# Layer 0 attention: softmax denominators of two key blocks in one four-band product, added and spread once per group of heads

## What is computed

```python
q = layer_norm(x) @ Wq                 # 16 heads of 64, 512 queries, 2 batches
k, v = split(layer_norm(ctx) @ Wkv)    # 1024 keys
k = apply_rope(k, cos, sin)
attn = softmax(q @ k.T * 64 ** -0.5)   # exp(scores) / sum over the 1024 keys
x = x + (attn @ v) @ Wo + bo
```

## Time and profile before

| | |
|---|---|
| runs | 3860.3, 3867.1, 3866.78 us; median 3866.78 us |
| the profiled execution | 3865.0 us, of which the span of the trace is 3863.3 us |
| TensorE (PE) busy | 2639.0 us, 68% of the span |
| VectorE busy | 2407.8 us, 62% |
| ScalarE busy | 1475.5 us, 38% |
| mean granted TensorE clock | 0.83 |
| TensorE in layer 0's attention, 91.1 to 610.9 us | 517.17 us busy of 519.80, clock 1.00 |

### The profile page before, as it was taken

One profiled execution on the slowest core, in us unless ns is written; L12 is line 12 of the kernel. 1 busy time (PEld: TensorE's weight loads), 2 busy tenths in 40 slices (PEclk: granted clock), 3 DMA queues, 4 the chain that ended last, 5 costly groups with the idle time before them and its releaser, 6 DMA issues. The chain is left out here.

```text
span 3863.3 us, 39157 instructions
## 1 busy us (share of the span) xinstructions
PE 2639.0 (68%) x11814; PEld 1688.4 (44%) x11814; DVE 2407.8 (62%) x4807; ACT 1475.5 (38%) x2242; POOL 320.4 (8%) x143
## 2 busy tenths in 40 slices
PE   2999996352433322234899995878768598499678
PEld 2444443230111111113788883545433587245367
DVE  4677663848777778873555453665555455587277
ACT  2444441116666766763222212222125122156221
POOL 0000000010000000000222210111110011200021
PEclk8999998575666656666999997889879798789789
DMA  1000000050000000000111101000041110522011
GB/s 56 13 12 13 11 6 35 0 178 6 22 23 23 1 23 22 22 1 32 49 49 49 41 14 41 1 0 0 10 134 42 37 43 17 183 48 67 19 37 35
DMA packets 46338, 136.44 MB, mean 35 GB/s; under 512 B 8568, under 2 KB 18816, under 8 KB 41600
## 3 DMA queue, kind: packets, MB, share of 16 engines
q1 hardware_dynamic: 46208, 135.01, 11.7%
HBM read 106.28 MB, written 28.31 MB: 35 GB/s over the span
## 5 line engine op out<-in xcount | busy, mean ns | idle before, releaser
L1403 ACT ACTIVATE l1a_over_s<-l1a_sc_s,l1a_ntau_s 128x1024 bf16<-128x1024 f32 x272 | 312.2, 1148 | 149.4 <-DVEq L1431 141.4
L1229 PE MATMUL ps<-ident,l1a_worst_s 128*1 128x128 f32 x8 | 3.0, 372 | 484.8 <-DVEq L1490 484.8
L1722 PE MATMUL ps<-m1e_x_part_s,m1e_up_part_s 128*128 128x512 f32 x1296 | 299.1, 392 | 22.0 <-POOL m1e_up_part_s L1818 15.9
L1284 DVE MAX8 l1a_cand_s<-ps 128x8 f32<-128x128 f32 x1024 | 218.4, 284 | 133.2 <-PE ps L1189 127.2
L1722 PEld LDWEIGHTS ps<-m1e_x_part_s,m1e_up_part_s 128*128 128x128 f32 x1296 | 244.5, 189 | 74.5 <-issue 23.7
L1189 PE MATMUL ps<-l1a_ka_s,l1a_qa_s 128*128 128x512 f32 x256 | 146.0, 590 | 110.9 <-ACT l1a_sc_s L1355 90.1
L1355 ACT ACTIVATE l1a_sc_s<-ps 128x512 f32<-128x512 f32 x256 | 153.0, 598 | 168.4 <-DVE l1a_cand_s L1284 168.4
L1229 PEld LDWEIGHTS ps<-ident,l1a_worst_s 128*1 128x1 f32 x8 | 0.6, 79 | 491.6 <-issue 428.7
L1765 ACT ACTIVATE m1e_act_out_s<-ps 128x512 f32<-128x512 f32 x108 | 64.6, 598 | 348.0 <-PE ps L1722 348.0
L973 DVE TENSOR_REDUCE l3a_shift_s<-ps 128x1 f32<-128x1024 f32 x128 | 150.1, 1219 | 65.5 <-PE ps L890 65.5
L543 DVE TENSOR_SCALAR l0a_probs_s<-l0a_probs_s 128x1024 f32<-128x1024 f32 x128 | 88.5, 691 | 150.3 <-ACT l0a_probs_s L610 149.9
(11 more groups left out here) (515 smaller groups left out, 5854.7 us busy)
## 6 DMA issues: line engine op xcount, KB each, us to landing
m1ew_up_s<-m_up SPq DMA_DIRECT2D x9, 1536.0 KB, 6.5
l1a_ka_s<-l_k_parts SPq DMA_DIRECT2D x16, 512.0 KB, 7.8
l3h_ka_s<-l_k_parts SPq DMA_DIRECT2D x16, 512.0 KB, 8.1
m1ew_down_s<-m_down SPq DMA_DIRECT2D x9, 768.0 KB, 4.3
l0a_w_s<-l_w SPq DMA_DIRECT2D x16, 384.0 KB, 3.0
m3ew_up_s<-m_up SPq DMA_DIRECT2D x6, 768.0 KB, 4.2
l_v_groups<-l1p_v_all_s SPq DMA_DIRECT2D x2, 2048.0 KB, 6.6
l1a_qa_s<-l_q_parts SPq DMA_DIRECT2D x16, 256.0 KB, 5.9
```

What stands on the lines that cost most here:

```text
L1284: ins = nc.vector.max(T["cand"][:, r, 8 * (c + j * 4):8 * (c + j * 4) + 8], ps[:, f % 2, c * P:(c + 1) * P])
L1403: nc.scalar.activation(T["over"][:, :], T["sc"][:, r, :], ACT.Relu, bias=T["ntau"][:, r:r + 1], accum_out=T["total"][:, r:r + 1]).then_inc ...
L1722: ins = nc.tensor.matmul(ps[:, 2 * (u % 2) + way, :], up_parts[a][:, k, way, c, :], x_parts[b][:, k, half * BANK:(half + 1) * BANK], start ...
```

## The change

A product with ones as weights is no longer made for each block, but for each second one. After the value product of an odd block t, four products with 32 columns each (L483 after) write four bands of 32 partitions of bank 7: block t-1 of head 0, block t-1 of head 1, block t of head 0, block t of head 1. At the group's end bank 7 holds for each head two partial sums, each 32 times. ScalarE copies it to `den` as before. Then a new product (`denominators`, L490 after) with the constant table `pair_sum` adds the two bands of a head and spreads the sum over the head's 64 partitions, into bank 7 again. It stands in step 2 of the next group, behind the value product of block 0 and ahead of the scores of block 3. The reciprocal reads bank 7 in place of `den`. Its step is FINISH_AT = 3 instead of 6. The value product of block 1, also in step 3, waits for this reciprocal (`rden_ready`), since the bank is written again behind it. The ring of `probs` has 8 places instead of 4, and `pv_done` is raised by two for each second block. `constants` makes `pair_sum` with one memset and two selects on GpSimd.

```diff
+            pool.memset(pair_sum[:, :], 0.0).then_inc(filled, 1)
...
+            both = pair_sum[:, :].rearrange("p (h c) -> p h c", h=2)
+            for part in range(2):
+                pool.wait_ge(made, 5 + part)
+                pool.affine_select(out=both, in_=both, compare_op=ALU.not_equal, fill=1.0, base=-64 * part,
+                                   pattern=[[-32, 2], [0, 64]], channel_multiplier=1).then_inc(made, 1)
...
-            dve.wait_ge(made, 5)
+            dve.wait_ge(made, 7)
...
-    SLOTS = 4
+    SLOTS = 8
...
-    LOW_QUERIES_AT, ROTATE_AT, LOW_KEYS_AT, FINISH_AT = 1, (2, 4), (5, 6), 6
+    LOW_QUERIES_AT, ROTATE_AT, LOW_KEYS_AT, FINISH_AT = 1, (2, 4), (5, 6), 3
...
                 if t == 0:
                     pe.wait_ge(v_ready, 2 * n + 4)
                     pe.wait_ge(o_copied, n + 1)
-                    pe.wait_ge(den_copied, n + 1)
+                if t == 1:
+                    pe.wait_ge(rden_ready, n + 1)
                 pe.wait_ge(clip_done, NC_ * n + t + 1 + SLOTS)
                 for h in range(2):
-                    nc.tensor.matmul(ps[64 * h:64 * h + 64, 6, :], v[:, p, t, 64 * h:64 * h + 64],
+                    ins = nc.tensor.matmul(ps[64 * h:64 * h + 64, 6, :], v[:, p, t, 64 * h:64 * h + 64],
                                      probs[:, t % SLOTS, h * NQ:(h + 1) * NQ], start=(t == 0), stop=(t == NC_ - 1))
-                for h in range(2):
-                    ins = nc.tensor.matmul(ps[64 * h:64 * h + 64, 7, :], ones[:, 0:64],
-                                           probs[:, t % SLOTS, h * NQ:(h + 1) * NQ], start=(t == 0), stop=(t == NC_ - 1))
-                ins.then_inc(pv_done, 1)
+                if t % 2 == 1:
+                    for i in range(4):
+                        ins = nc.tensor.matmul(ps[32 * i:32 * i + 32, 7, :], ones[:, 0:32],
+                                               probs[:, (t - 1 + i // 2) % SLOTS, i % 2 * NQ:(i % 2 + 1) * NQ],
+                                               start=(t == 1), stop=(t == NC_ - 1))
+                    ins.then_inc(pv_done, 2)
+
+            def denominators(n):
+                pe.wait_ge(den_copied, n + 2)
+                nc.tensor.matmul(ps[:, 7, :], pair_sum[:, :], den[:, :], start=True, stop=True).then_inc(den_made, 1)
...
+                    if last is not None and t == 2:
+                        denominators(n - 1)
                 if after is None:
                     value_product(n, p, NC_ - 2)
                     value_product(n, p, NC_ - 1)
+                    denominators(n)
...
                 dve.wait_ge(o_done, n + 1)
-                dve.wait_ge(den_copied, n + 2)
-                nc.vector.reciprocal(rden[:, :], den[:, :]).then_inc(rden_ready, 1)
-                dve.wait_ge(rden_ready, n + 1)
+                dve.wait_ge(den_made, n + 1)
+                nc.vector.reciprocal(rden[:, :], ps[:, 7, :]).then_inc(rden_ready, 1)
+                dve.wait_ge(rden_ready, n + 2)
```

More of the change, by code:

```diff
@@ L94, in link, with constants @@
         self.wait()
-def constants(nc, ident, ones, slot_sum, slot_pick, spread):
+def constants(nc, ident, ones, slot_sum, slot_pick, spread, pair_sum):
     with Stage(nc, "const") as s:
@@ L111, in _ @@
             pool.memset(spread_f32[:, :], 0.0).then_inc(filled, 1)
-            pool.wait_ge(filled, 5)
+            pool.memset(pair_sum[:, :], 0.0).then_inc(filled, 1)
+            pool.wait_ge(filled, 6)
             pool.affine_select(out=ident[:, :], in_=ident[:, :], compare_op=ALU.not_equal, fill=1.0, base=0,
@@ L343, in _, with rope_attention @@
             dve.wait_ge(added, TQ)
-def rope_attention(nc, name, ps, ones, q_t, ctx_t, w_dram, cos_dram, sin_dram, o_all):
+def rope_attention(nc, name, ps, ones, pair_sum, q_t, ctx_t, w_dram, cos_dram, sin_dram, o_all):
     DH = 64
@@ L390, in rope_attention @@
         pv_done = s.sem("pv_done")
-        o_copied, den_copied = s.sem("o_copied"), s.sem("den_copied")
+        o_copied, den_copied, den_made = s.sem("o_copied"), s.sem("den_copied"), s.sem("den_made")
         rden_ready, o_done = s.sem("rden_ready"), s.sem("o_done")
@@ L467, in value_product @@
                     pe.wait_ge(o_copied, n + 1)
-                    pe.wait_ge(den_copied, n + 1)
+                if t == 1:
+                    pe.wait_ge(rden_ready, n + 1)
                 pe.wait_ge(clip_done, NC_ * n + t + 1 + SLOTS)
                 for h in range(2):
-                    nc.tensor.matmul(ps[64 * h:64 * h + 64, 6, :], v[:, p, t, 64 * h:64 * h + 64],
+                    ins = nc.tensor.matmul(ps[64 * h:64 * h + 64, 6, :], v[:, p, t, 64 * h:64 * h + 64],
                                      probs[:, t % SLOTS, h * NQ:(h + 1) * NQ], start=(t == 0), stop=(t == NC_ - 1))
-                for h in range(2):
-                    ins = nc.tensor.matmul(ps[64 * h:64 * h + 64, 7, :], ones[:, 0:64],
-                                           probs[:, t % SLOTS, h * NQ:(h + 1) * NQ], start=(t == 0), stop=(t == NC_ - 1))
-                ins.then_inc(pv_done, 1)
+                if t % 2 == 1:
[7 more added lines that the diff above has]
+                nc.tensor.matmul(ps[:, 7, :], pair_sum[:, :], den[:, :], start=True, stop=True).then_inc(den_made, 1)
             def first():
                 for sem, free in ((w_free, 2), (v_ready, 2), (exp_done, 2), (clip_done, SLOTS), (pv_done, SLOTS),
-                                  (o_copied, 1), (den_copied, 1), (o_done, 1)):
+                                  (o_copied, 1), (den_copied, 1), (o_done, 1), (rden_ready, 1)):
                     nc.tensor.sem_inc(sem, free)
@@ L2510, in build @@
         slot_pick, spread = sb("slot_pick", [P, 60]), sb("spread", [P, 6, P], F32R)
+        pair_sum = sb("pair_sum", [P, P])
         x = sb("x_rows", [P, TQ, D])
@@ L2515, in by_feature @@
             return A[name + "_f"]
-        constants(nc, ident, ones, slot_sum, slot_pick, spread)
+        constants(nc, ident, ones, slot_sum, slot_pick, spread, pair_sum)
         load_x(nc, A["x"], x)
@@ L2555, in build @@
                 o_all = sb("l0_o_all", [P, 8, NT], stack=l0)
-                rope_attention(nc, "l0a", ps, ones, q_t, c_t, A["l0_w"], A["l0_cos"], A["l0_sin"], o_all)
+                rope_attention(nc, "l0a", ps, ones, pair_sum, q_t, c_t, A["l0_w"], A["l0_cos"], A["l0_sin"], o_all)
                 project_out(nc, "l0o", ps, o_all, 8, A["l0_wo"], A["L0_xattn_bo"], x)
```

## The result

The changed kernel takes 3973.96 us (median; 3971.59 to 3977.46), the kernel before, on the same chip, 3865.1 us: a ratio of 1.0284 with a 95% interval of 1.0266 to 1.0302. The forecast was 3980 us.

A forecast was written before the change was run, and what follows sets the result against it. TensorE was taken to bound layer 0's attention. TensorE savings -39.6, new wait +113, slow clock +38 and the rest +1.7 sum to +113 us: 3980 us, 2.9% more, range 3940 to 4000.

The forecast's parts named there:

- the bands: TensorE's denominator products, layer 0 attention: 64 dropped in even blocks save 58.2 us, 64 four-band ones in odd blocks lose 5.8.
- the slow clock: TensorE behind each stop: mean 5.1 us at half pace, 2.6 us lost per gap, +38 us in all.
- spread product, 15 in the stage: TensorE's product adding the bands and spreading the sum: 0.85 us each, 15 inside the stage, +12.8 us.
- TensorE's stop: Value product of block 1 waits for VectorE's reciprocal: 7.7 us in groups 1 to 14, 5.2 in group 15, +113 us.
- constants and the last spread: GpSimd's memset and two selects, 0.7 us, and the last group's bare spread product, 1.0 us: together +1.7 us.
- nothing else is late: The second rotation's result is ready before TensorE asks in step 6, 10.1 against 12.4 us after restart: no second wait.
- Rival (a): After TensorE's stall the clock stays at 2.4 GHz, so the wait costs less: 3942 us; chance 0.10.
- price of a change of band width: On TensorE, 0.05 us more where one product's band width differs from the next one's.
- estimate of 1.08 us for four bands: A four-band product's time from the notes' 2.38 times for three bands; sum 6 us higher; forecast used the trace's 0.99.
- Rival (b): TensorE never feels the wait because the reciprocal is done by 233: faster, 3829 us; chance 0.05.
- turning point: The stall at which faster turns to slower: 2.4 us a group, clock included.
- Rival (c): The four bands don't run together, each pair taking its own 0.91 us: +58 us, 4038 us; chance 0.03.

The follow-up runs named there:

- bands alone: The changed kernel without spread product and new wait, bands copied and reciprocal in step 6, a head's two partial sums not added: 3825.58 us, 0.9892 of before.
- stop filled: The changed kernel with eight extra unneeded 128x512 products in TensorE's wait, groups 1 to 15: 3952.16 us, 1.0225 of before.
- earlier reciprocal: The changed kernel with reciprocal and its multiplication behind the clip of block 2, ahead of the first rotation on VectorE: 3883.48 us, 1.0046 of before.
- later wait: The changed kernel with the wait for the reciprocal moved from the value product of block 1 to the denominator product behind it: 3965.04 us, 1.0255 of before.
- bunched version: The changed kernel with denominator products of four blocks together behind blocks 3 and 7, the wait there, reciprocal in step 3: 3829.85 us, 0.9917 of before.
- narrow product alone: The kernel before with each denominator product of two 64-column bands written as four of 32, nothing merged: 3885.0 us, 1.0047 of before.
- copying versions: The changed kernel with ScalarE copying bank 7 out, the wait on that copy, reciprocal in step 6: 3834.4 us; also with four blocks' denominators together: 3833.15 us.
- half of the stop filled: The changed kernel with four extra unneeded products in TensorE's wait, 4.2 us of idle time left: 3977.97 us, 1.0287 of before.

## Why the prediction was right

The direction, the place, the mechanism and the size came out. Two terms were off, the bands by 10 us and the slow clock by 8.5, in opposite senses: that the total came within 6 us of the median is in part luck, though either error alone would have left it inside the range.

| term | forecast | measured |
|---|---|---|
| bands (even blocks less, odd blocks more) | -52.4 | -42.4 (bands alone, stage end) |
| spread product, 15 in the stage | +12.8 | +12.9 (0.86 each) |
| TensorE's stop | +113 | +111.4 |
| slow clock behind it | +38 | +29.5 (stop filled) |
| constants and the last spread | +1.7 | +2.2 (1.0 and 1.23) |
| the stage | +113 | +113.6 from the parts, +114.9 in the trace |

- **The stop** was the main step, and it held in each piece: 7.60 us for 7.7 in the groups of the loop, 5.2 for 5.2 in the last, 15 times, and none in the first. It came from laying out VectorE's instructions behind the end of the query projection. The earlier reciprocal (2.67 us left), the later wait (6.52) and the bunched version (no stop) confirm it: each moved the stop by what the chain said. That nothing else is late held too: the second rotation made no wait.
- **The slow clock**: the step was right, its size not. The 5.1 us at half pace were a mean from another stage; here they are about 4.5 in the rows shown, and the filled stop gives 2.0 us a stop, not 2.6. Rival (a), that the clock holds, fell: no stop of the changed kernel was free of it.
- **The bands**: the mis-sized term is the price of a change of band width. I took the 0.05 us between the 0.91 and the 0.96 of the earlier trace rows for it. But these are two products, each followed by another kind. Measured on one and the same value product it is 0.10, and it falls on all 128 blocks, where the forecast had 0.05 on each: 6.4 of the 10 us. An even block saves 0.86 for 0.91, an odd one costs 0.14 for 0.09, and the narrow product alone came to 0.14 each. Another 2 us are the 0.14 us a group that came with the eight slots; the last 1 to 2 us stay open. The Trainium skill, TensorEngine Tiling (Array Packing), section Tiling Modes, says that a change of tiling mode drains TensorE. The longer step at a change of width agrees with it in direction; whether the array ran empty no run shows, and the 0.14 of an odd block stayed below the 0.25 that I had put for a full emptying. The estimate of 1.08 us for four bands, from the 2.38 times for three in the Trainium skill, TensorE: Matmul & The Clock Gate, section Part 3, wasn't met. Four bands took 0.99 to 1.00 us, as the earlier trace rows had it.
- **Rival (b)**, faster since the wait is never felt, was no property of this change: it needed the wait moved. Where the wait is met, in the bunched and in the copying versions, the bands do give 31 to 35 us. Its turning point was too high. With the measured terms (-42.4 + 12.9 + 2.2 = -27.3 us) gain and loss balance at 1.8 us a stop, clock included, not at 2.4; the earlier reciprocal, with 2.67 us and 0.4 of slow clock, was 18 us slower. **Rival (c)** fell: 8 records in 1.00 us.
- The median rose by 109 us and the stage by 115. The difference lies in the rest of the program, in which no instruction was changed. By the traces it scatters between 3238.5 and 3258.4 us, and one trace is one execution: the runs of a single kernel already lie up to 15 us apart (the bunched one: 3827.5 to 3843.0). What makes it scatter was not tried.

## What to carry to other kernels

Before a buffer is given a new reader, look at where that reader's engine will be, not at how long the reader takes: here 3.4 us of reciprocal became a stop of 7.6 us of the bounding engine, since it stood behind 5 us of other work that hangs on the bounding engine itself. A wait that a slower engine releases belongs as late in the bounding engine's queue as the buffer allows (or the buffer is emptied by an idle engine); that alone turned +2.8% into -0.8%. Price an idle gap of TensorE with the slow stretch behind it. Here that was 2.0 us for each gap, whether it was 7.6 or 4.2 us long; at 2.6 us it was spared 12 times in 15.

## What the runs showed of the hardware

- The length of a gap alone doesn't decide whether the clock falls. Of 15 gaps of 2.6 us three ended at 1.2 GHz; of 14 gaps of 4.2 us, eleven ended slow and in three the clock fell 1.2 to 1.3 us after work had begun again. The key projection at the program's start, which had kept 2.4 GHz after 3.40 us, was slow in the changed kernel after 3.25 us and fast in the kernel with half of the stop filled after 3.60 (3.78 and 1.98 us for the same four records):

```profile
77.26 3.78 PE L445 MATMUL ps<-l_c_t,l0a_w_s 128*128 128x512 f32 x4 [3.25 <-DVE l0a_q_lo_s L527]
...
78.68 1.98 PE L447 MATMUL ps<-l_c_t,l0a_w_s 128*128 128x512 f32 x4 [3.60 <-DVE l0a_q_lo_s L533]
```

- The step from one product to another of a different band width costs 0.10 us over the same width (1.01 for 0.91 us, value products of 64 columns, 32-bit).
- With a register addition between a wait and the product behind it, that product began 0.14 us later (2.34 for 2.20 us from the value projection to the scores). That the addition is the cause was not tried by itself.
